# First block of an adaptive-norm layer on one core: conditioning load moved to ScalarE's queue, two engines for the first evacuations, gate product ahead of the low rank product

## Chip, cores, metric

One Trainium2 chip, one core. The metric is the device time of one execution in microseconds (us); lower is better. A time is the median over several executions, and beside it one execution is profiled.

## What is computed

A transformer layer on 2048 tokens of width 256 in float32: a modulation vector from the conditioning vector `c`, gated linear attention, then a mixture of 8 experts with 2 per token and a shared expert. Cut to what bears on the change:

```python
mod = (silu(c) @ wmod).reshape(2, 6, 1, -1)          # c: 2 x 256, wmod: 256 x 1536
sa, ca, ga, sb, cb, gb = mod[:, 0], ..., mod[:, 5]
h = layernorm(x) * (1 + ca) + sa                      # x: 2 x 1024 x 256
q, k, v = h @ Wq, h @ Wk, h @ Wv
gk = log_sigmoid(h @ Wg1 @ Wg2 + bg2) / 16            # low rank: 256 -> 16 -> 256
o = scan over chunks of 64 tokens with decay exp(cumsum(gk))
o = rmsnorm(o) * silu(h @ Wgate)
x = x + ga * (o @ Wo)
h = layernorm(x) * (1 + cb) + sb
x = x + gb * (top-2 experts of h + gated shared expert of h)
```

## The kernel before, in words

It is written by hand, engine by engine: each engine has its own list of instructions in a fixed order, and semaphores tie the lists together. Nothing schedules at run time, and each engine takes its list strictly in order.

The attention half runs over four blocks of 512 tokens (s = 0 to 3; channels lie on the partitions, in two halves of 128, and tokens on the free axis). The change touches only what comes ahead of and in block 0:

- SyncE's queue issues the loads: `x` of block 0 (L439), the conditioning vector into `csb` (L440), the first 512 columns of `wmod` into `hs` (L441), then the small weights `wg` (L444 to L448), `wgate`, `wv`, `wk`, `wq` (L452) and so on.
- TensorE starts with 14 products of a matrix of ones (`idle_products`, L1534), whose results nobody reads. Then `mod_cols` (L1544) makes the modulation columns, `transpose_x` (L1676, XT) turns the normalised rows, three more products of ones follow, and then, in the order of the list: `low_rank` (L1685, LR), the first half of the gate product (L1526, G 0), `gate_logits` (L1693, Z), the second half of the gate product (L1526, G 1), the first half of the values (L1667, V), keys (K), queries (Q), `mod_rows` (L1553), the second half of the values, `key_rows` (L1706), the transposes of block 1.
- ScalarE makes `csil`, the silu of the conditioning vector (L712), the rstd of the layer norm (L726, L728), evacuates both halves of the transposed rows to `hT` with scale and shift (`evac_xT`, L769), evacuates LR to `tT` (L783), takes |z| of Z (L789), softplus (L794, L796), loads the silu table (L718), evacuates G to `sg` (L853), loads another table (L715), evacuates values (L760), makes the gate's exponentials (L802, L806), the normalised rows of block 1 (L775), evacuates `mod_rows` (L734), values (L760), `ktok` (L902), and then `hT` of block 1 (L769).
- VectorE computes statistics (L1065 to L1070), the normalised rows `xn` (L1079), the modulation columns (L1094, L1095), then min(z, 0) (L1207), the log of the gate and its running sum (L1212 to L1219), twice, the statistics of block 1, `kh` (L1326), `nmr` of block 1 (L1333), the queries times the gate (L1340).

Eight PSUM banks are given out by a fixed list, `unit_order`. A unit (XT, LR, G, Z, ...) is one use of a bank; TensorE counts `unit_full` up when it has filled one, in the order of that list, and waits ahead of a unit for what `released` names for the unit that had the bank before. Banks 0 and 1 of the list are `work`, 2 and 3 are `at_ps2` and `at_ps3`, 4 and 5 are `at_ps0` and `at_ps1`.

Of the kernel before, what the change touches and what calls it, by code (L numbers as in the profile page):

```python
# [19 lines left out]
ALU = mybir.AluOpType  # L20
ACT = mybir.ActivationFunctionType
AX_X = mybir.AxisListType.X

P = 128
# [8 lines left out]
KC = HID // P  # L33
# [31 lines left out]
BANKS = {("G", 0): 0, ("G", 1): 1, ("V", 0): 0, ("HT", 0): 0, ("HT", 1): 0, ("K", 0): 1, ("RT", 0): 0, ("RX", 0): 0, ("K", 1): 2,  # L65
         ("Q", 0): 3, ("Q", 1): 1, ("V", 1): 0, ("KT", 0): 2, ("KT", 1): 3, ("XT", 0): 1, ("XT", 1): 0, ("WO", 0): 2,
         ("LR", 0): 3, ("WO", 1): 1, ("Z", 0): 2, ("Z", 1): 3}
# [2 lines left out]
MASK_ORDER = (2, 3, 0, 1)  # L70


FIRST_BANKS = {("V", 0): 4, ("K", 0): 5}


TAIL_BANKS = {1: (3, 2), 2: (4, 5), 3: (0, 1), 4: (3, 2), 5: (4,)}


def unit_order():
    units = [(("MODC", 0, 0), 2), (("XT", 0, 0), BANKS["XT", 0]), (("XT", 0, 1), BANKS["XT", 1])]  # L80
    ring = [2]

    def put(kind, blk, j):
        own = FIRST_BANKS if blk == 0 else {}
        units.append(((kind, blk, j), own.get((kind, j), BANKS[kind, j])))

    def turn(*keys):
        for key in keys:
            units.append((key, (units[-1][1] + 1) % ring[-1]))

    def part(kind, blk, i):
        turn(*([("SD", blk, 0), ("SD", blk, 1)] if kind == "D" else [("SA", blk, i)] + [("SB", blk, i)][:i < FTS - 1]))

    def fill(s, place):
        for kind, blk, i in FILL.get((s, place), ()):
            part(kind, blk, i)

    put("LR", 0, 0)
    put("G", 0, 0)
    put("Z", 0, 0)  # L100
    put("Z", 0, 1)
    put("G", 0, 1)
    for s in range(NBLK):
        b, h = s - 1, s - 2
        if s:
            put("G", s, 0)
            put("G", s, 1)
        put("V", s, 0)
        put("K", s, 0)
        if h >= 0:  # L110
            put("HT", h, 0)
        put("K", s, 1)
        if h >= 0:
            put("HT", h, 1)
            put("RT", h, 0)
        put("Q", s, 0)
        if h >= 0:
            put("RX", h, 0)
        for kind, j in (("Q", 1), ("V", 1), ("KT", 0), ("KT", 1)):
            put(kind, s, j)  # L120
        if s + 1 < NBLK:
            put("XT", s + 1, 0)
            put("XT", s + 1, 1)
        if b >= 0:
            put("WO", b, 0)
        if s + 1 < NBLK:
            put("LR", s + 1, 0)
            put("Z", s + 1, 0)
            put("Z", s + 1, 1)
        if b >= 0:  # L130
            put("WO", b, 1)
    fill(NBLK, "gates")
    fill(NBLK, "half")
    turn(("HT", NBLK - 2, 0), ("HT", NBLK - 2, 1), ("RT", NBLK - 2, 0))
    fill(NBLK, "second")
    turn(("RX", NBLK - 2, 0), ("RK", 0, 0))
    ring.append(4)
    fill(NBLK, "norm")
    turn(("WO", NBLK - 1, 0), ("WO", NBLK - 1, 1))
    fill(NBLK, "stats")  # L140
    fill(NBLK, "ln")
    turn(("HT", NBLK - 1, 0), ("HT", NBLK - 1, 1))
    fill(NBLK, "transposed")
    turn(("RT", NBLK - 1, 0), ("RX", NBLK - 1, 0))
    fill(NBLK, "top2")
    fill(NBLK, "scatter")
    for f in range(EARLY_UP, FTS):
        units += [((kind, NBLK - 1, f), TAIL_BANKS[f][n]) for n, kind in enumerate(("SA", "SB")[:1 + (f < FTS - 1)])]
    units += [(("SD", NBLK - 1, n), n) for n in range(2)]
    return units  # L150
# [25 lines left out]
def adaln_moe(nc, x, cT, wmod, wq, wk, wv, wg1, wg2, bg2, wgate, norm_w, wo,  # L176
              router, e_up, e_down, s_up, s_down, out):
    with ExitStack() as ctx:
# [6 lines left out]
        def sem(name):  # L185
            return ctx.enter_context(nc.semaphore(name))
# [7 lines left out]
        at_ps = [ps(f"at_ps{j}", [P, 512]) for j in range(NPAIR)]  # L194
        o_ps = [ps("o_even", [P, 512]), ps("o_odd", [P, 512])]
# [150 lines left out]
        xs_zero = sem("xs_zero")  # L346
        ones_ready = sem("ones_ready")
        const_pool, ident_ready, zero_ready, kv_full = sem("const_pool"), sem("ident_ready"), sem("zero_ready"), sem("kv_full")
        modf_ready, mod_stored, ld_rows = sem("modf_ready"), sem("mod_stored"), sem("ld_rows")
        unit_full, modr_full, nmr_ready, ld_modr = sem("unit_full"), sem("modr_full"), sem("nmr_ready"), sem("ld_modr")  # L350
        dve_step, act_step, pool_step = sem("dve_step"), sem("act_step"), sem("pool_step")
# [38 lines left out]
        def released(key):  # L390

            kind, blk, j = key
            return {
                "MODC": [(modc_ready, 2)],
                "XT": [(ht_ready, 2 * blk + j + 1)],
                "LR": [(tt_ready, blk + 1)],
                "Z": [(zabs_done, 2 * blk + j + 1), (zmin_done, 2 * blk + j + 1)],
                "G": [(sg_ready, 2 * blk + j + 1)],
                "V": [(v_ready, 2 * blk + j + 1)],
                "K": [(kh_ready, 2 * blk + j + 1)],  # L400
                "WO": [(woev_done, 2 * blk + j + 1)],
                "Q": [(qeo_ready, 4 * blk + 2 * j + 2)],
                "KT": [(ktok_ready, 2 * blk + j + 1)],
                "HT": [(h2T_ready, 2 * blk + j + 1)],
                "RT": [(rt_ready, blk + 1)],
                "RX": [(logit_ready, blk + 1)],
                "RK": [(rank_read, 2)],
                "SA": [(silu_done, FTS * blk + j + 1)] if j < FTS - 1 else [(hs_ready, FTS * blk + j + 1)],
                "SB": [(hs_ready, FTS * blk + j + 1)],
                "SD": [(shev_done, 2 * blk + j + 1)],  # L410
            }[kind]

        def bank(key):
            return (work + at_ps[2:] + at_ps[:2])[BANK_OF[key]]

        def wait_unit(eng, key):

            eng.wait_ge(unit_full, TURN[key] + 1)
# [18 lines left out]
        @block.sync  # L437
        def _(sp):
            sp.dma_start(x_sb[:, 0:TPB, :], x[0:BLK, :].rearrange("(t p) c -> p t c", p=P)).then_inc(ld_x[0], 16)  # L439
            sp.dma_start(csb[:, :, :], cT).then_inc(ld_c, 16)  # L440
            sp.dma_start(wmod_sb[:, :, 0:2 * HID], wmod.rearrange("(k p) n -> p k n", p=P)[:, :, 0:2 * HID]  # L441
                         ).then_inc(ld_mod, 16)
            sp.wait_ge(zero_ready, 4)
# [264 lines left out]
        def _(act):  # L708
            a = nc.scalar
            steps = Steps(act, act_step)  # L710
            act.wait_ge(ld_c, 16)
            a.activation(csil[:, :, :], csb[:, :, :], ACT.Silu).then_inc(csil_ready, 1)  # L712

# [51 lines left out]
            def evac_xT(s):  # L765
                row = s // BPB
                for k in range(KC):
                    wait_unit(act, ("XT", s, k))
                    a.activation(hT[:, k, :], bank(("XT", s, k))[:, :], ACT.Identity,  # L769
                                 bias=cols[:, 0, k, row:row + 1], scale=cols[:, 1, k, row:row + 1]).then_inc(ht_ready, 1)  # L770
# [64 lines left out]
                a.activation(dtop[:, tl, :], dtop[:, tl, :], ACT.Copy).then_inc(pexp_ready, 1)  # L835

            act.wait_ge(modc_ready, 2)
            evac_xT(0)
            evac_low_rank(0)
            z_abs(0)  # L840
            for s in range(NBLK + 1):
# [216 lines left out]
        def _(dve):  # L1058
# [201 lines left out]
            def next_state(s):  # L1260
# [17 lines left out]
                if s >= 1:  # L1278
# [3 lines left out]
                                     kv_in[:, :, :, :].rearrange("p g v c -> p (g v c)"), 0.0,  # L1282
                                     ALU.mult, ALU.add).then_inc(state_ready, 1)

            dve.wait_ge(const_pool, 1)
            z_min(0)
            for s in range(NBLK + 1):
# [225 lines left out]
        def _(pe):  # L1513
            t_ = nc.tensor

            def begin(key):

                if LAST_IN_BANK[key]:
                    for s, val in released(LAST_IN_BANK[key]):
                        pe.wait_ge(s, val)  # L1520
                return bank(key)

            def project(key, w, gr, rhs):
                o = begin(key)
                for k in range(KC):
                    ins = t_.matmul(o[:, :], w[:, k, gr * P:(gr + 1) * P], rhs[:, k, :],  # L1526
                                    start=(k == 0), stop=(k == KC - 1))
                ins.then_inc(unit_full, 1)


            def idle_products(n):

                for _ in range(n):
                    t_.matmul(at_ps[0][:, 0:P], ones[:, :], ones[:, :], start=True, stop=True)  # L1534

            def mod_cols():
                pe.wait_ge(csil_ready, 1)
# [139 lines left out]
                    ins.then_inc(unit_full, 1)  # L1677

            def low_rank(s):
                pe.wait_ge(ht_ready, 2 * s + 2)  # L1680
                o = begin(("LR", s, 0))
                for gr in range(KC):
                    for k in range(KC):
                        r = slice(32 * (2 * gr + k), 32 * (2 * gr + k) + 32)
                        ins = t_.matmul(o[r, :], wg1_sb[:, k, :], hT[:, k, :], start=True, stop=True)  # L1685
                ins.then_inc(unit_full, 1)
# [54 lines left out]
            mod_cols()  # L1741
            transpose_x(0)
            idle_products(3)
            pe.wait_ge(ld_wg, 16 * (NPAIR + 3))
            low_rank(0)
            pe.wait_ge(ld_wgate, 16)
            project(("G", 0, 0), wgate_sb, 0, hT)
            gate_logits(0)
            project(("G", 0, 1), wgate_sb, 1, hT)
            for s in range(NBLK + 1):  # L1750
                b, h = s - 1, s - 2
                if b >= 0:
# [237 lines left out]
```

## Times and profile before

| what | value |
|---|---|
| median of 3 runs | 378.75 us (377.57 to 380.47) |
| profiled execution, its own time | 378.7 us |
| its span, first to last instruction | 376.9 us |
| what lies around the span | 1.8 us |
| TensorE busy | 360.6 us, 96% of the span |
| VectorE busy | 237.4 us, 63% |
| ScalarE busy | 144.6 us, 38% |
| GpSimd busy | 147.7 us, 39% |
| chain that ended last, by engine | TensorE 79%, VectorE 12%, ScalarE 5%, issue 3% |
| granted TensorE clock, mean | 0.999 of 2.4 GHz |

The busy shares are averages over the whole kernel. The change acts in the first 31 us, and what it is worth is read there: what each engine waits for in that stretch, and what hands over to the next block.

### The profile page before, as it was taken

Reading aid. Unit: us, or ns where it says so; the run is one execution under the profiler, and the core shown is the slowest. Engines: PE = TensorE matmul, PEld = TensorE weight load, DVE = VectorE, ACT = ScalarE, POOL = GpSimd, SP = SyncE. Lnnn points to the kernel's source line nnn. Section 1 sums busy time; section 2 is a strip of 40 time slices with the busy share of each in tenths; the row PEclk is TensorE's granted clock in tenths of the full one; section 3 lists DMA queues with packets and bytes.
Section 4 is the critical chain, followed back from the end, with each engine's and each line's share of the span. In section 5 each row is a group of like instructions: output and inputs, shape, how many; then the busy total and the mean of one; then the engine's idle time right before and its main releaser. Section 6 shows DMA issues by size and latency. Waiting matters only on the chain.

```text
span 376.9 us, 10005 instructions
## 1 busy us (share of the span) xinstructions
PE 360.6 (96%) x3871; PEld 226.8 (60%) x3872; DVE 237.4 (63%) x578; ACT 144.6 (38%) x303; POOL 147.7 (39%) x253
## 2 busy tenths in 40 slices
PE   8999989989899989899999999999999999999994
PEld 8445656665665564556744844756666666665463
DVE  4199576996799479664491771165565555555295
ACT  3597556716681613271052411024333333331110
POOL 7705007101510242026270075333667666675100
PEclk9999999999999999999999999999999999999999
DMA  6970200000000000069920082422333333211495
GB/s 204 337 236 27 92 4 3 2 5 3 2 2 5 2 2 4 3 175 333 297 99 14 1 213 80 124 72 87 107 93 111 113 102 92 70 57 44 154 353 172
DMA packets 29902, 36.68 MB, mean 97 GB/s; under 512 B 4567, under 2 KB 26530, under 8 KB 29860
## 3 DMA queue, kind: packets, MB, share of 16 engines
q1 hardware_dynamic: 26452, 27.58, 24.2%
q0 software_dynamic: 3408, 8.51, 6.7%
q8 instruction: 30, 0.49, 0.5%
q14 instruction: 12, 0.10, 0.1%
HBM read 23.31 MB, written 13.68 MB: 98 GB/s over the span
## 4 chain that ended last, share of the span: by engine, by line
PE 79%; DVE 12%; ACT 5%; issue 3%; DVEq 0%; POOL 0%; ACTq 0%; POOLq 0%
PE at_ps L1864 13%; PE work L1477 10%; PE at_ps L1477 8%; PE at_ps L1492 6%; PE work L1887 4%; PE at_ps L1526 4%; PE work L1492 3%; PE work L1889 3%; PE work L1526 2%; PE at_ps L1848 2%; PE at_ps L1699 2%; DVE arena L1227 2%; PE at_ps L1534 2%; PE at_ps L1717 2%; PE work L1667 2%
## 5 line engine op out<-in xcount | busy, mean ns | idle before, releaser
L678 POOL DMA_INDIRECT ys_tokens<-er_pos,goal_u x39 | 42.1, 1080 | 33.8 <-DVE er_pos L1400 27.2
L1864 PE MATMUL at_ps<-arena 128*128 x156 | 54.5, 472 | 0.0
L649 POOL DMA_INDIRECT xs_sorted<-h2tok,pos_u x32 | 31.9, 997 | 37.2 <-DVE pos_u L1024 18.8
L607 POOL TENSOR_TENSOR sq<-sq,sg 128x512 f32<-128x512 f32 x8 | 10.0, 1274 | 88.8 <-issue 88.8
L1864 PEld LDWEIGHTS at_ps<-arena 128*128 128x128 f32 x156 | 26.6, 190 | 14.9 <-issue 6.6
L930 ACT ACTIVATE arena<-at_ps 128x176 f32<-128x176 f32 x39 | 12.4, 318 | 58.8 <-PE at_ps L1864 58.8
L1400 DVE SCALAR_TENSOR_TENSOR er_pos<-work,goal,sq 128x256 f32<-128x256 f32 x39 | 17.2, 480 | 22.0 <-PE work L1894 21.0
L1477 PE MATMUL work<-h2T,sup_sb 128*128 128x512 f32 x56 | 25.7, 598 | 0.2 <-ACT hs L699 0.2
L1380 DVE TENSOR_TENSOR arena<-at_ps,arena 128x176 f32<-128x176 f32 x39 | 13.3, 342 | 18.4 <-ACT arena L930 15.9
L1227 DVE COPY_PREDICATED arena<-causal,at_ps 128x512 f32<-128x512 uint32 x32 | 20.5, 720 | 4.0 <-PE at_ps L1564 4.0
L1492 PE MATMUL at_ps<-sdn_sb,hs 128*128 128x256 f32 x100 | 22.1, 380 | 0.0
L1123 DVE TENSOR_TENSOR hs<-work,hs 128x512 f32<-128x512 f32 x12 | 8.3, 689 | 20.6 <-PE work L1477 20.6
L1492 PEld LDWEIGHTS at_ps<-sdn_sb,hs 128*128 128x128 f32 x100 | 18.9, 190 | 3.4 <-issue 1.0
L699 ACT ACTIVATE hs<-at_ps 128x512 f32<-128x512 f32 x9 | 5.4, 597 | 39.9 <-PE at_ps L1477 39.9
L926 ACT ACTIVATE arena<-at_ps 128x256 f32<-128x256 f32 x39 | 14.9, 384 | 9.7 <-PE at_ps L1848 9.3
L1477 PEld LDWEIGHTS work<-h2T,sup_sb 128*128 128x128 f32 x56 | 10.3, 190 | 12.2 <-issue 11.8
L1393 DVE SCALAR_TENSOR_TENSOR sq<-sq,goal,rows 128x256 f32<-128x256 f32 x40 | 17.4, 478 | 0.0
L1848 PEld LDWEIGHTS at_ps<-ident,h2tok 128*128 128x128 f32 x78 | 10.8, 141 | 10.0 <-issue 6.1
L1526 PE MATMUL work<-hT,wgate_sb 128*128 128x512 f32 x32 | 14.9, 602 | 0.0
L1848 PE MATMUL at_ps<-ident,h2tok 128*128 128x128 f32 x78 | 14.8, 273 | 0.0
L611 POOL TENSOR_TENSOR arena<-arena 128x512 f32<-128x512 f32 x8 | 10.2, 1283 | 11.6 <-DVE arena L1340 11.4
L1667 PE MATMUL work<-wv_sb,hT 128*128 128x256 f32 x56 | 13.6, 386 | 0.5 <-ACT sg L853 0.5
(287 smaller groups left out, 815.0 us busy)
## 6 DMA issues: line engine op xcount, KB each, us to landing
h2tok<-xs_sorted SPq DMA_DIRECT2D x40, 131.5 KB, 2.1
arena<-ys_tokens SPq DMA_DIRECT2D x8, 512.0 KB, 7.4
arena<-in_e_up SPq DMA_DIRECT2D x8, 352.0 KB, 5.4
x_sb<-in_x SPq DMA_DIRECT2D x4, 512.0 KB, 8.5
out_rows<-x_sb SPq DMA_DIRECT2D x16, 128.0 KB, 4.2
sup_sb<-in_s_up SPq DMA_DIRECT2D x2, 640.0 KB, 4.9
xs_sorted<-state SPq DMA_DIRECT2D x2, 526.0 KB, 14.4
xs_sorted<-state SPq DMA_DIRECT2D x8, 131.5 KB, 4.3
```

The lines of the kernel that those rows point to most:

```text
L649: g.indirect_dma_start(out=xs_dram, out_offset=bass.IndirectOffsetOnAxis(ap=pos_u[:, k, t:t + 1], axis=0), in_=h2tok[:, t, :], in_offset=N ...
L678: g.indirect_dma_start(out=ys_dram, out_offset=bass.IndirectOffsetOnAxis(ap=goal_u[:, i:i + 1], axis=0), in_=yout[:, q % 2, u, :], in_offs ...
L1227: v.copy_predicated(atm[:, n % 2, j, :], causal[:, :, :].bitcast(U32).rearrange("p r l -> p (r l)"), at_ps[j][:, :]).then_inc(atm_ready, 1)
L1393: v.scalar_tensor_tensor(out=row_gain[:, t, :], in0=row_step, scalar=goal[:, (u // 2) % XPAIRS, t, 2:3], in1=rows[:, 0, GB, :], op0=ALU.mu ...
L1400: v.scalar_tensor_tensor(out=yout[:, (u // 2) % 2, u % 2, :], in0=work[u % 2][:, 0:HID], scalar=goal[:, (u // 2) % XPAIRS, u % 2, 1:2], in ...
L1477: ins = t_.matmul(o[0:m, :], sup_sb[:, k, w, f0:f0 + m], h2T_of[blk][:, k, :], start=(k == 0), stop=(k == KC - 1))
L1492: t_.matmul(o[jj][:, t * HID:(t + 1) * HID], hs[:, f, tk], sdn_sb[:, f, :], start=(t == 0 and f == 0), stop=False, skip_group_check=True)
L1526: ins = t_.matmul(o[:, :], w[:, k, gr * P:(gr + 1) * P], rhs[:, k, :], start=(k == 0), stop=(k == KC - 1))
L1667: ins = t_.matmul(o[:, t * HID:(t + 1) * HID], hT[:, k, tk], wv_sb[:, k, :], start=(k == 0), stop=(k == KC - 1))
L1848: ins = t_.transpose(at_ps[u % 2][:, k * P:(k + 1) * P], xt[:, u // 2, u % 2, k * P:(k + 1) * P], ident[:, :])
L1864: ins = t_.matmul(at_ps[2 + u % 2][:, 0:2 * FE], xT[:, u % 2, k * P:(k + 1) * P], eup[:, bass.ds(e, 1), k, :].rearrange("p a n -> p (a n)" ...
L1887: t_.matmul(work[t][:, 0:HID], hTe[:, w % 2, t * P:(t + 1) * P], main[:, bass.ds(e[t], 1), :].rearrange("p a n -> p (a n)"), start=True, s ...
```

## The change

Five things are edited. (1) The load of the conditioning vector leaves SyncE's queue and becomes ScalarE's first instruction. (2) The transposes of block 0 go to banks 4 and 5 (`at_ps0`, `at_ps1`), and the products of ones write `o_ps[1]`. (3) Channel half 0 of `hT` is evacuated by ScalarE as before, half 1 by VectorE, each with a semaphore of its own (`ht_first`). (4) TensorE makes G 0 first, each of its two matmuls waiting for its own half of `hT`, then LR. (5) G 1 now stands between LR and Z, where G 0 stood. The counts of `ht_ready` are lowered by two, since block 0 no longer raises it.

```diff
-FIRST_BANKS = {("V", 0): 4, ("K", 0): 5}
+FIRST_BANKS = {("V", 0): 4, ("K", 0): 5, ("XT", 0): 4, ("XT", 1): 5}
...
+    put("G", 0, 0)
     put("LR", 0, 0)
-    put("G", 0, 0)
+    put("G", 0, 1)
     put("Z", 0, 0)
     put("Z", 0, 1)
-    put("G", 0, 1)
...
-                "XT": [(ht_ready, 2 * blk + j + 1)],
+                "XT": [(ht_ready, 2 * blk + j - 1) if blk else (ht_first[j % KC], 1)],
...
-            sp.dma_start(csb[:, :, :], cT).then_inc(ld_c, 16)
...
+            act.dma_start(csb[:, :, :], cT).then_inc(ld_c, 16)
             act.wait_ge(ld_c, 16)
...
             act.wait_ge(modc_ready, 2)
-            evac_xT(0)
+            wait_unit(act, ("XT", 0, 0))
+            a.activation(hT[:, 0, :], bank(("XT", 0, 0))[:, :], ACT.Identity,
+                         bias=cols[:, 0, 0, 0:1], scale=cols[:, 1, 0, 0:1]).then_inc(ht_first[0], 1)
...
+            dve.wait_ge(modc_ready, 2)
+            wait_unit(dve, ("XT", 0, 1))
+            v.tensor_scalar(hT[:, 1, :], bank(("XT", 0, 1))[:, :], cols[:, 1, 1, 0:1], cols[:, 0, 1, 0:1],
+                            ALU.mult, ALU.add).then_inc(ht_first[1], 1)
             dve.wait_ge(const_pool, 1)
...
-                    t_.matmul(at_ps[0][:, 0:P], ones[:, :], ones[:, :], start=True, stop=True)
+                    t_.matmul(o_ps[1][:, 0:P], ones[:, :], ones[:, :], start=True, stop=True)
...
-                pe.wait_ge(ht_ready, 2 * s + 2)
+                if s:
+                    pe.wait_ge(ht_ready, 2 * s)
...
             idle_products(3)
+            pe.wait_ge(ld_wgate, 16)
+            o = begin(("G", 0, 0))
+            for k in range(KC):
+                pe.wait_ge(ht_first[k], 1)
+                ins = t_.matmul(o[:, :], wgate_sb[:, k, 0:P], hT[:, k, :], start=(k == 0), stop=(k == KC - 1))
+            ins.then_inc(unit_full, 1)
             pe.wait_ge(ld_wg, 16 * (NPAIR + 3))
             low_rank(0)
-            pe.wait_ge(ld_wgate, 16)
-            project(("G", 0, 0), wgate_sb, 0, hT)
+            project(("G", 0, 1), wgate_sb, 1, hT)
             gate_logits(0)
-            project(("G", 0, 1), wgate_sb, 1, hT)
```

TensorE's list behind the transposes, before; `wg1_sb` marks LR, `wgate_sb` the gate product, `tT` Z:

```order
L1534 MATMUL at_ps0<-ones 128x128 x3
L1685 MATMUL at_ps3<-hT,wg1_sb 32x512 [waits ht_ready,ld_wg]
L1685 MATMUL at_ps3<-hT,wg1_sb 32x512 x3
L1526 MATMUL work0<-hT,wgate_sb 128x512 [waits ht_ready,ld_wgate]
L1526 MATMUL work0<-hT,wgate_sb 128x512
L1693 MATMUL at_ps2<-tT,wg2_sb 128x512 [waits tt_ready,modc_ready]
L1693 MATMUL at_ps3<-tT,wg2_sb 128x512
L1526 MATMUL work1<-hT,wgate_sb 128x512 [waits ht_ready]
L1526 MATMUL work1<-hT,wgate_sb 128x512
```

The same place in the changed kernel, down to the first product of the values:

```order
L1541 MATMUL o_odd<-ones 128x128 x3
L1756 MATMUL work0<-hT,wgate_sb 128x512 [waits ht_first0,ld_wgate]
L1756 MATMUL work0<-hT,wgate_sb 128x512 [waits ht_first1]
L1693 MATMUL at_ps3<-hT,wg1_sb 32x512 [waits ld_wg]
L1693 MATMUL at_ps3<-hT,wg1_sb 32x512 x3
L1533 MATMUL work1<-hT,wgate_sb 128x512 x2
L1701 MATMUL at_ps2<-tT,wg2_sb 128x512 [waits tt_ready,modc_ready]
L1701 MATMUL at_ps3<-tT,wg2_sb 128x512
L1674 MATMUL at_ps0<-wv_sb,hT 128x256 [waits ht_first0,ld_wv]
```

Between the evacuation of the transposes and Z stood four matmuls of LR and two of the gate product; now four of LR and four of the gate product stand there.

VectorE's list at the same place, before:

```order
L1094 COPY cols<-at_ps2 128x4 [waits unit_full,dve_step]
L1095 TENSOR_SCALAR cols<-at_ps2 128x4
L1207 TENSOR_SCALAR gate_pair<-at_ps2 128x512 [waits zabs_done,unit_full,const_pool]
L1207 TENSOR_SCALAR gate_pair<-at_ps3 128x512 [waits zabs_done,unit_full]
L1212 TENSOR_TENSOR gate_pair<-gate_pair,za 128x512 [waits zmin_done,zln_done]
```

And in the changed kernel:

```order
L1097 COPY cols<-at_ps2 128x4 [waits unit_full,dve_step]
L1098 TENSOR_SCALAR cols<-at_ps2 128x4
L1290 TENSOR_SCALAR hT<-at_ps1,cols 128x512 [waits unit_full,modc_ready]
L1210 TENSOR_SCALAR gate_pair<-at_ps2 128x512 [waits zabs_done,unit_full,const_pool]
L1210 TENSOR_SCALAR gate_pair<-at_ps3 128x512 [waits zabs_done,unit_full]
L1215 TENSOR_TENSOR gate_pair<-gate_pair,za 128x512 [waits zmin_done,zln_done]
```

One instruction is added, between the modulation columns and the first work on Z.

## Rows read from the trace of the kernel before

**Rows 1.** Chain that ended last, first 33 us: start us, us, what
```profile
1.02 6.32 PE at_ps L1534 x28
...
26.76 1.94 PE work L1667 x8
...
28.72 0.66 ACT arena L760 x2
...
30.36 1.34 ACT hT L769 x2
...
31.75 1.11 PE at_ps L1685 x8
```

**Rows 2.** Timeline 6.5 to 17 us: start, us, engine, line, operation, count [idle before]
```profile
6.95 1.99 PEld L1544 LDWEIGHTS at_ps<-csil,hs 128*128 128x128 f32 x16
...
7.06 1.43 DVE L1079 TENSOR_SCALAR xn<-x_sb,rstd,nmr 128x256 f32<-128x256 f32 x4
...
8.89 1.07 PE L1676 MATMUL work<-ident,xn 128*128 128x128 f32 x8
...
9.62 1.45 ACT L769 ACTIVATE hT<-work,cols 128x512 f32<-128x512 f32 x2 [2.79 <-PE work L1676]
...
11.21 1.06 PE L1685 MATMUL at_ps<-hT,wg_sb 128*32 128x512 f32 x8 [0.58 <-ACT hT L769]
...
12.21 1.98 PE L1526 MATMUL work<-hT,wgate_sb 128*128 128x512 f32 x4
...
14.12 1.13 PE L1693 MATMUL at_ps<-tT,wg_sb 64*128 64x512 f32 x4
...
15.18 1.98 PE L1526 MATMUL work<-hT,wgate_sb 128*128 128x512 f32 x4
15.28 1.09 ACT L789 ACTIVATE za<-at_ps 128x512 f32<-128x512 f32 x2 [2.26 <-PE at_ps L1693]
...
17.00 1.89 PE L1667 MATMUL at_ps<-wv_sb,hT 128*128 128x256 f32 x8
```

**Rows 3.** Waits of ScalarE, all there are from 16.2 to 32 us: in total, times, longest
```profile
ACT xn L775 <- DVE nmr L1333: 0.6, 1, 0.6
ACT arena L760 <- PE work L1667: 0.2, 1, 0.2
```

**Rows 4.** Timeline of VectorE (first row) and ScalarE, 15 to 32 us
```profile
18.58 0.69 DVE L1212 TENSOR_TENSOR gate_pair<-gate_pair,za 128x512 f32<-128x512 f32 x1 [1.28 <-ACT za L796]
...
26.22 2.08 ACT L775 ACTIVATE xn<-x_sb,nmr,rstd 128x256 f32<-128x256 f32 x4 [0.59 <-DVE nmr L1333]
...
28.20 0.36 ACT L734 ACTIVATE yT<-o_even 128x256 f32<-128x256 f32 x1
...
28.72 0.66 ACT L760 ACTIVATE arena<-work 128x256 f32<-128x256 f32 x2 [0.16 <-PE work L1667]
```

**Rows 5.** Line L1207 alone, 15 to 18 us: duration ns min/median/max
```profile
L1207 DVE TENSOR_SCALAR gate_pair<-at_ps x2: 679/685/691, 16.0 to 16.6; 128x512 f32<-128x512 f32 x2
```

**Rows 6.** Timeline 0 to 7 us: what waits for the first loads
```profile
4.22 1.40 DVE L1065 BATCH_NORM_STATS2 stats<-x_sb 128x6 f32<-128x256 f32 x4 [4.22 <-DMA x_sb<-in_x]
...
4.43 0.20 ACT L712 ACTIVATE csil<-csb 128x4 f32<-128x4 f32 x1 [2.38 <-DMA csb<-in_cT]
...
6.29 0.30 ACT L726 ACTIVATE lnv<-mv,eps_c 128x4 f32<-128x4 f32 x1 [0.35 <-DVE mv L1070]
```

**Rows 7.** DMA issues of the first 8 us: engine, count, KB, us to landing
```profile
hs<-in_wmod SPq DMA_DIRECT2D x1, 512.0 KB, 5.0
```

**Rows 8.** Timeline: SyncE's queue at its second and third issue
```profile
1.27 0.49 SPq L440 DMA_DIRECT2D csb<-in_cT  x1
...
1.82 0.43 SPq L441 DMA_DIRECT2D hs<-in_wmod  x1
```

**Rows 9.** Stretches: length; busy us (instructions) by engine; clock; DMA share; GB/s
```profile
3.00:4.00 1.00, 1.00 (x7) 1.00 (x7) 0.00 (x0) 0.00 (x0) 0.93 (x4) 1.00 1.04 293
...
17.00:30.00 13.00, 13.00 (x63) 7.84 (x62) 11.37 (x26) 12.13 (x25) 2.35 (x2) 1.00 0.69 201
```

More of the change, by code:

```diff
@@ L70 @@
 MASK_ORDER = (2, 3, 0, 1)
-FIRST_BANKS = {("V", 0): 4, ("K", 0): 5}
+FIRST_BANKS = {("V", 0): 4, ("K", 0): 5, ("XT", 0): 4, ("XT", 1): 5}
 TAIL_BANKS = {1: (3, 2), 2: (4, 5), 3: (0, 1), 4: (3, 2), 5: (4,)}
 def unit_order():
-    units = [(("MODC", 0, 0), 2), (("XT", 0, 0), BANKS["XT", 0]), (("XT", 0, 1), BANKS["XT", 1])]
+    units = [(("MODC", 0, 0), 2), (("XT", 0, 0), 4), (("XT", 0, 1), 5)]
     ring = [2]
@@ L348, in adaln_moe @@
         const_pool, ident_ready, zero_ready, kv_full = sem("const_pool"), sem("ident_ready"), sem("zero_ready"), sem("kv_full")
+        ht_first = [sem("ht_first0"), sem("ht_first1")]
         modf_ready, mod_stored, ld_rows = sem("modf_ready"), sem("mod_stored"), sem("ld_rows")
```

## Prediction

> **What bounds the kernel now.** I read the chain that ended last first, and only its first 32 us, since nothing behind block 0 is edited. It begins on TensorE with the products of ones, is TensorE at the end of the second half of the values (26.76 + 1.94 = 28.70 us), and there it passes to ScalarE: values, `ktok`, `hT` of block 1, done at 31.70 us, and LR of block 1 starts at 31.75 [rows 1]. A reader of the chain alone would say: TensorE bounds block 0, so whatever starts TensorE sooner is gained.
>
> The second view is the list of waits from 16.2 to 32 us, and it says how thin that reading is. ScalarE's wait for TensorE at the handover is 0.16 us; its only other one is for VectorE's `nmr`, 0.59 us, and VectorE's last one is for ScalarE's softplus (1.28 us, over at 18.58) [rows 3, 4]. In the stretch 17 to 30 us TensorE is busy for 13.00 of 13.00 us, ScalarE for 12.13 and VectorE for 11.37 [rows 9]. So there are two strings of nearly equal length through block 0. One is TensorE's own queue. The other starts at Z: |z| on ScalarE at 15.28, right behind Z's end at 15.25, two softplus steps, VectorE at 18.58, straight on to `nmr`, then ScalarE's rows of block 1 (26.22 to 28.30), `mod_rows` (to 28.56), and then the handover at 28.72 [rows 2, 4]. The second string is only 0.16 us shorter than the first. It hangs on when Z is done, not on when TensorE is done.
>
> **The change part by part.**
>
> *Conditioning load on ScalarE's queue.* SyncE issues `wmod` at about 1.27 instead of 1.82 us [rows 8]: 0.55 us sooner. Before, it lands at 1.82 + 5.0 = 6.8 us [rows 7, 8], while the weight loads of the 14 products of ones (28 instructions) hold TensorE's queue from 1.02 to 6.95 us, 5.93 / 28 = 0.212 us each with no gap, and the modulation product's first weight load follows at 6.95 [rows 1, 2]. The queue hides the landing, and it is unchanged in length: 0 us gained (an earlier landing would count only with fewer products of ones ahead of it). The issue on ScalarE (0.49 us on SyncE [rows 8]) stands ahead of its table load; `csil` was made at 4.43, and ScalarE then had 0.35 us to spare ahead of `lnv` [rows 6]. The vector would have to land 0.35 us later than now to cost anything, and it is issued about 0.5 us sooner. 0 us.
>
> *Evacuation by two engines.* ScalarE took 9.62 to 11.07 for both halves, and LR started at 11.21, 0.14 us behind [rows 1, 2]. One half alone is (1.45 us for two that overlap a little) about 0.77 us, done at 10.39 to 10.41. VectorE's half has no row; the nearest is its 128x512 read of PSUM in L1207, 0.685 us [rows 5]. The second transpose ends at 9.96 [rows 2], VectorE has been idle since the modulation columns, so half 1 is done at about 10.7. Bounds of this operation: 0.68 us if the two scalars per partition cost nothing, 0.77 us as on ScalarE; in both cases it is done ahead of 11.3 us, when TensorE wants it (below). So the first product can start at 10.40 + 0.14 = 10.55 us, 0.66 us sooner than LR did.
>
> *G 0 ahead of LR, G 1 ahead of Z.* TensorE's starts are the prices: LR 11.21 to 12.21 = 1.00 us, G 0 12.21 to 14.12 = 1.91, Z 14.12 to 15.18 = 1.06, G 1 15.18 to 17.00 = 1.82 [rows 2]. From the first product to Z's start it was 1.00 + 1.91 = 2.91 us. Now it is 1.91 + 1.00 + 1.91 = 4.82. A full-width product followed by LR (four strips of 32 columns) has no row here; bounds are 1.82 (full width followed by full width) and 1.91 (full width followed by Z), and I take 1.91. So:
>
> - Z starts at 10.55 + 4.82 = 15.37 instead of 14.12: **1.25 us later**. `tT` is no bound: LR ends at 12.46 + 1.06 = 13.5, and an evacuation of the size of ScalarE's 0.77 us makes 14.3.
> - V starts at 15.37 + 1.06 = 16.43 instead of 17.00: **0.57 us sooner**. All four units are still ahead of it, so this is the 0.66 us less 0.09 for one more change of shape.
>
> *Where both arrive.* TensorE's string is at the handover 0.57 us sooner, at 28.13. The other string is 1.25 us later all along: |z| at 16.53, VectorE at 19.83, the rows of block 1 27.47 to 29.55, `mod_rows` to 29.81, and so values at about 29.83 instead of 28.72. The 0.16 us wait for TensorE is gone and is all the slack there was: 1.25 - 0.16 + 0.02 = **1.1 us later**. Everything behind it, `ktok`, `hT`, LR of block 1, is ScalarE at work without a pause, and TensorE waits there for it already [rows 1]. What else is late next: TensorE's transposes of block 1 need the rows of block 1, which are done at 29.55, and take 1.07 us as in block 0 [rows 2], so they end at 30.7, while ScalarE wants the first of them at 30.36 + 1.1 = 31.5. Hidden by 0.8 us.
>
> *Behind block 0.* The order there is the same, each block starts from the last one's `hT`, and the loads it needs were early. I take the 1.1 us to pass to the end. Sum against the profiled execution: 376.9 + 1.1 = 378.0 us of span, 379.8 of time; that execution (378.7) lies at the median (378.75), so **379.85 us**.
>
> *New banks, one semaphore for each half.* V's first half now waits for the bank of the transposes, free since 10.4, at 16.4: 0 us. G 0 no longer has a unit ahead of it in its bank. 0 us.
>
> **The rivals.**
>
> 1. *TensorE's string sets the end (faster).* If the string behind Z had as much slack as it loses, 1.25 us, block 0 would end with TensorE, 0.57 us sooner: 378.2 us. For it: the chain names TensorE up to 28.70, and TensorE is the engine that is never idle. Against it: waits of 0.16 and 0.59 us are all that the trace shows, and the 0.59 us is ScalarE waiting for VectorE, on the same string. It decides from a slack of about 1.1 us on.
> 2. *The delay is absorbed further on (no change).* Blocks 2 and 3 and the expert half have stretches in which TensorE's queue is full; a later handover in block 1 may meet one that is bound by TensorE work which is not late. For it: 96% busy. Against: the chain passes through ScalarE from 28.72 to 31.70 [rows 1], so TensorE's own queue is pushed back by the 1.1 us at that point. 378.8 us.
> 3. *The first rows land later (slower still).* From 3 to 4 us the DMA engines are busy all the time (share 1.04), and VectorE's first work waits for `x` at 4.22 [rows 6, 9]. From `x` the way goes to `xn`, done at 7.06 + 1.43 = 8.49, and the transposes start at 8.89 [rows 2], right behind the modulation products, so 0.40 us are to spare. With `wmod` 0.55 us sooner beside it, `x` can be late by up to 0.55 us, and 0.15 us would be left; if the transposes' weight loads are what the rows must meet, 0.1 us more: 380.1 us.
>
> The Trainium skill, page "DMA: Bandwidth & Descriptors", section "Issuing engines are not separate DMA queues", says that transfers issued by different engines run on the same 16 DMA engines and interleave, and that a second issuing engine only saves the time of the issue. By that rule the move takes nothing off the transfers and can hold up `x`, as the third rival has it; by the rows alone the move is worth 0.
>
> **How the numbers follow.** Forecast (0.7 to 1.6 us slower, 379.45 to 380.35): 0.60. Rival 1: 0.12. Rival 2: 0.15. Rival 3: 0.13. The three runs before span 377.57 to 380.47, so a median moves by some 0.8 us by itself. The range goes from 378.0 (takes in most of rivals 1 and 2) to 381.2 (rival 3 and 1 us of spread). All cases lie within 1% (3.8 us), which is about what a measurement of this kernel can tell from no change; only a mechanism that I don't see would leave it: faster 0.02, within 1% 0.94, slower 0.04.
>
> **What would show it.** In the profile after: G 0 starts at about 10.55 us and runs into its second matmul without a pause; Z starts at about 15.4; |z| at about 16.5; V at about 16.4; ScalarE's second evacuation of values (L760's) at about 29.8, with no wait for TensorE ahead of it, and the chain going from there back through `mod_rows`, the rows of block 1, VectorE and softplus to Z instead of through TensorE; LR of block 1 at about 32.85 instead of 31.75. The prediction is wrong if ScalarE still waits for TensorE at that handover, if Z starts before 15 us, or if LR of block 1 is late by 1.1 us and the span isn't.

## The result, and the profile after

The changed kernel takes 379.9 us (median of 19 runs, 378.46 to 381.77), the kernel before 378.57 us in 19 runs beside it: ratio 1.0034, 95% interval 1.0019 to 1.0049. A second set gave 379.87 against 378.57 us, ratio 1.0030 (1.0011 to 1.0050). The change makes the kernel 1.3 us slower, 0.34%; 379.85 was forecast.

| profiled execution | before | after |
|---|---|---|
| span | 376.9 us | 380.0 us |
| TensorE busy | 360.6 us | 362.6 us |
| VectorE busy | 237.4 us | 237.8 us |
| ScalarE busy | 144.6 us | 143.8 us |
| mean granted TensorE clock, of 2.4 GHz | 0.999 | 0.993 |
| chain by engine | PE 79%, DVE 12%, ACT 5% | PE 74%, DVE 14%, ACT 6% |

This one execution is longer by 3.1 us, more than the medians, and its clock column says why to look twice. The timeline of the changed kernel, as in [rows 2, 6] (start us, length us, engine, line, operation, [idle before, releaser]):

```profile
0.78 0.44 ACTq L711 DMA_DIRECT2D csb<-in_cT  x1
...
4.75 1.41 DVE L1068 BATCH_NORM_STATS2 stats<-x_sb 128x6 f32<-128x256 f32 x4 [4.75 <-DMA x_sb<-in_x]
...
6.48 1.85 PE L1551 MATMUL at_ps<-csil,hs 128*128 128x2 f32 x16
...
9.03 1.92 PE L1683 MATMUL at_ps<-ident,xn 128*128 128x128 f32 x8 [0.71 <-DVE xn L1082]
...
12.02 2.14 PE L1756 MATMUL work<-hT,wgate_sb 128*128 128x512 f32 x4
...
17.00 1.13 PE L1701 MATMUL at_ps<-tT,wg_sb 64*128 64x512 f32 x4
...
18.06 1.99 PE L1674 MATMUL at_ps<-wv_sb,hT 128*128 128x256 f32 x8
```

`x` lands at 4.75 instead of 4.22 us; TensorE is through with its modulation products at 8.33 and has nothing to do until 9.03, when `xn` is there; and the transposes take 1.92 us, where they took 1.07. The stretches around it (length, busy time and count of each engine, granted clock, DMA share, GB/s):

```profile
8.00:9.00 1.00, 0.32 (x3) 0.23 (x3) 1.00 (x6) 0.00 (x0) 0.83 (x3) 1.00 0.69 176
9.00:10.00 1.00, 0.97 (x5) 0.97 (x6) 0.11 (x2) 0.00 (x0) 0.84 (x4) 0.56 1.09 372
```

From 9.1 us on the clock is granted at 1.2 GHz (0.50 in the half microseconds from 9.5 to 12), behind TensorE's pause. This comes ahead of the first product whose place was changed, so the new order didn't cause it, and it isn't in every execution: of the changed kernel's 19 runs 14 have a mean clock of 0.993 to 0.997 (median span 378.3 us), five have 0.998 or more (376.9 us).

The other half is as forecast. The waits from 16 to 33 us, to be held against [rows 3]:

```profile
PE work L1683 <- DVE arena L1347: 0.8, 1, 0.8
ACT xn L776 <- DVE nmr L1340: 0.6, 1, 0.6
```

ScalarE no longer waits for TensorE at the handover. TensorE waits there, for VectorE, and the chain that ended last goes through ScalarE and VectorE where it went through TensorE [rows 1]:

```profile
17.07 1.11 PE at_ps L1701 x4
18.18 1.07 ACT za L790 x2
...
28.91 0.16 DVE nmr L1340
29.10 2.08 ACT xn L776 x4
31.17 0.27 ACT yT L735
31.44 0.54 ACT arena L761 x2
31.98 0.97 ACT xn L905 x2
32.95 1.35 ACT hT L770 x2
34.34 1.11 PE at_ps L1693 x8
```

LR of block 1 starts at 34.34 instead of 31.75 us, 2.59 us later.

### The profile page after: what moved, and what is told of

Same layout as the page of the kernel before. It is cut to its first block, busy times and chain, and to the rows that moved or that the text cites. A ratio compares the mean times of both kernels' runs of the same rounds, so it can differ in the third digit from the quotient of the medians.

```text
span 380.0 us, 10007 instructions
## 1 busy us (share of the span) xinstructions
PE 362.6 (95%) x3871; PEld 227.7 (60%) x3872; DVE 237.8 (63%) x579; ACT 143.8 (38%) x302; POOL 147.7 (39%) x253
## 4 chain that ended last, share of the span: by engine, by line
PE 74%; DVE 14%; ACT 6%; issue 4%; DMA 1%; DVEq 0%; ACTq 0%
PE at_ps L1876 13%; PE work L1484 10%; PE at_ps L1484 8%; PE at_ps L1499 6%; PE work L1899 4%; PE work L1499 3%; PE work L1901 3%; PE at_ps L1533 2%; PE at_ps L1860 2%; PE at_ps L1707 2%; DVE arena L1230 2%; DVE stats L1068 2%; PE at_ps L1725 2%; PE work L1533 1%; PE o_even L1627 1%
## 5 line engine op out<-in xcount | busy, mean ns | idle before, releaser
L1068 DVE BATCH_NORM_STATS2 stats<-x_sb 128x6 f32<-128x256 f32 x32 | 11.2, 411 | 4.9 <-DMA x_sb<-in_x 4.7
```

The lines of the kernel that those rows point to most:

```text
L1068: steps.did(v.bn_stats(stats[:, which, t, :], x_sb[:, tile0 + t, :]))
```

## The experiments

There were twelve experiments, in three sets (e1 to e4, e5 to e8, e9 to e12); some are the same kernel a second time. Those of one set share a chip and the runs of the kernel before beside them (medians 378.25, 378.57 and 378.13 us), and each ratio is to these. "17" means 17 instead of 14 products of ones ahead of the modulation products. The last two columns sort the executions by their mean granted clock, as printed to three places; they carry much of what follows. The mean doesn't say where the clock fell; only the profiles do. In some profiles it is also at half in the last one or two microseconds of the span, behind the last product, where it costs nothing.

| kernel | load on | evacuation | order | ones | median us | spans with clock 0.998+ | with less |
|---|---|---|---|---|---|---|---|
| before, three sets | SyncE | ScalarE | old | 14 | 378.1 to 378.6 | 376.0 to 376.1 (54 of 96) | 377.0 to 377.5 (42 of 96) |
| changed, first runs | ScalarE | two | new | 14 | 379.90 | 376.9 (5 of 19) | 378.3 (14 of 19) |
| e5_changed_again | ScalarE | two | new | 14 | 379.87 | 376.6 (4 of 9) | 378.3 (5 of 9) |
| e1_load_only | ScalarE | ScalarE | old | 14 | 378.21 | 376.2 (7 of 12) | 377.2 (5 of 12) |
| e2_no_load | SyncE | two | new | 14 | 378.78 | 376.7 (8 of 12) | 378.35 (4 of 12) |
| e3_split_only | SyncE | two | old | 14 | 377.88 | 375.7 (8 of 12) | 377.3 (4 of 12) |
| e4_more_ones | ScalarE | two | new | 17 | 378.28 | 376.4 (12 of 12) | none |
| e9_changed_17 | ScalarE | two | new | 17 | 378.54 | 376.7 (12 of 12) | none |
| e10_split_load_17 | ScalarE | two | old | 17 | 377.06 | 375.3 (12 of 12) | none |
| e7_split_17 | SyncE | two | old | 17 | 377.04 | 375.25 (6 of 6) | none |
| e11_split_17_again | SyncE | two | old | 17 | 376.70 | 374.9 (12 of 12) | none |
| e6_before_17 | SyncE | ScalarE | old | 17 | 377.30 | 375.5 (12 of 12) | none |
| e12_before_17_again | SyncE | ScalarE | old | 17 | 377.24 | 375.4 (12 of 12) | none |
| e8_z_last | SyncE | ScalarE | LR, G 0, G 1, Z | 17 | 378.79 | 377.0 (11 of 12) | 378.0 (1 of 12) |

**e1_load_only.** The kernel before with one edit:

```diff
-            sp.dma_start(csb[:, :, :], cT).then_inc(ld_c, 16)
...
+            act.dma_start(csb[:, :, :], cT).then_inc(ld_c, 16)
             act.wait_ge(ld_c, 16)
```

> The kernel before, with only the load of the conditioning vector moved to ScalarE's queue. Theory A (a late x and a slow clock): x of block 0 lands at about 4.7 us instead of 4.2, TensorE stands idle ahead of the transposes for about 0.5 to 0.7 us, in most executions its clock then falls to 1.2 GHz for a while, the first LR starts later than 11.21 us by 0.2 (clock kept) to 1.4 us (clock lost), and the time is 0.2 to 1.3 us above that of the kernel before. Theory B (only the order of the products costs anything, as the prediction had it): LR starts at 11.2 us and the time is that of the kernel before within 0.2 us.

Measured: 378.21 us, ratio 0.9997 (0.9979 to 1.0015). Its profile has `x` at 4.29 us, no pause of TensorE, and LR at 11.16. By itself the move costs nothing that these runs can tell, as the prediction had it; the products of ones ran until 7.3 us in this execution, so the landing of `wmod` stayed hidden behind them.

**e2_no_load.** The changed kernel with the load back on SyncE's queue.

> The changed kernel, with the conditioning vector's load back on SyncE's queue. Theory B, the prediction's own sum: first gate product at 10.55 us, Z at 15.37 us, LR of block 1 at 32.85 us (before: 31.75), time 1.1 us above that of the kernel before. Theory A: the whole loss of the changed kernel comes from the late x and the clock, so LR of block 1 starts at 31.75 us or sooner and the time is at most that of the kernel before.

Measured: 378.78 us, ratio 1.0014 (0.9993 to 1.0036): half of the loss, with an interval that reaches both theories. Where the clock holds its span is 376.7 against 376.1 us, and that speaks against theory A: something is lost with the clock held, too. Its profile shows a second way into the same trouble (timeline of TensorE, then a stretch):

```profile
7.07 1.92 PE L1551 MATMUL at_ps<-csil,hs 128*128 128x2 f32 x16 [0.46 <-DMA hs<-in_wmod]
8.84 1.77 PE L1683 MATMUL at_ps<-ident,xn 128*128 128x128 f32 x8
```

```profile
9.00:10.00 1.00, 1.00 (x7) 1.00 (x7) 0.23 (x2) 0.14 (x1) 0.92 (x3) 0.53 0.82 192
```

Here the products of ones end at 6.6 us, TensorE waits 0.46 us for `wmod`, and the clock falls at 9 us. So the loss of clock doesn't need the moved load. LR of block 1 started at 34.12 in this profile, 2.37 us later than in the kernel before; held against 32.57 in e5 below, where the clock held, about 1.55 us of that are the slow stretch.

**e3_split_only.** The changed kernel with the load on SyncE's queue and the old order of products, LR waiting for both halves. TensorE's list, `+` marking what the kernel before hasn't got:

```diff
+            for k in range(KC):
+                pe.wait_ge(ht_first[k], 1)
             low_rank(0)
             pe.wait_ge(ld_wgate, 16)
             project(("G", 0, 0), wgate_sb, 0, hT)
             gate_logits(0)
             project(("G", 0, 1), wgate_sb, 1, hT)
```

> Only the two-engine evacuation and its banks: the vector's load on SyncE's queue and the products in the order of the kernel before (LR, G 0, Z, G 1). Theory B: LR of block 0 waits for VectorE's half, starts at about 10.85 us instead of 11.21, everything behind it shifts by the same 0.36 us (Z at 13.76, LR of block 1 at 31.4), time 0.36 us below that of the kernel before. Rival: TensorE's three products of ones behind the transposes, or the second evacuation, keep LR at 11.1 us or later, and nothing is gained.

Measured: 377.88 us, ratio 0.9982 (0.9957 to 1.0007). Where the clock holds its span is 375.7 against 376.1 us. The sign is as expected, but the interval of the ratio includes no change at all; e11's profile tells more. The profile of e3 is one of those with a fall of the clock.

**e4_more_ones.** The changed kernel, `idle_products(14)` made `idle_products(17)`.

> The changed kernel, with 17 instead of 14 products of ones ahead of the modulation products, about 0.64 us more of work at 2.4 GHz, to fill the pause in which TensorE waited for xn in the changed kernel's profile (8.3 to 9.03 us). Theory A (the pause costs the clock): the granted clock stays at 1.00 behind 9 us, the first gate product starts at 10.7 us or so instead of 12.02, and the time falls by about 1 us against the changed kernel's 1.3 us above before. Rival (the fall of the clock has nothing to do with this pause): the clock falls as often, and three more products change nothing or add up to 0.3 us.

Measured: 378.28 us, ratio 0.9990 (0.9972 to 1.0008). None of its 12 executions has a clock under 0.998, where 19 of 28 of the changed kernel have. Its first gate product starts at 10.96 us instead of 12.02, and its transposes start right behind the modulation products. With three more products, and no pause ahead of the transposes, the clock holds; whether it is the missing pause or the added work that holds it, no run tells apart.

**e5_changed_again.**

> The changed kernel once more, on the chip of the runs beside it, since its single profile had a fall of TensorE's clock at 9 us. If the fall is a matter of chance that the change makes likelier, most executions have a mean granted clock of 0.993 to 0.996 and a span of about 378.3 us, the others 0.998 to 1.000 and about 376.9. Time 1.0 to 1.5 us above before.

Measured: 379.87 us, ratio 1.0030 (1.0011 to 1.0050): five executions of nine with the lower clock, four without. Its profile fell among those where the clock held, and so is the one to check the prediction's times by. Timeline:

```profile
4.50 1.41 DVE L1068 BATCH_NORM_STATS2 stats<-x_sb 128x6 f32<-128x256 f32 x4 [4.50 <-DMA x_sb<-in_x]
...
6.08 1.92 PE L1551 MATMUL at_ps<-csil,hs 128*128 128x2 f32 x16 [0.21 <-DMA hs<-in_wmod]
...
8.77 1.09 PE L1683 MATMUL at_ps<-ident,xn 128*128 128x128 f32 x8 [0.77 <-DVE xn L1082]
...
10.45 1.95 PE L1756 MATMUL work<-hT,wgate_sb 128*128 128x512 f32 x4
...
15.24 1.13 PE L1701 MATMUL at_ps<-tT,wg_sb 64*128 64x512 f32 x4
16.30 1.99 PE L1674 MATMUL at_ps<-wv_sb,hT 128*128 128x256 f32 x8
16.40 1.09 ACT L790 ACTIVATE za<-at_ps 128x512 f32<-128x512 f32 x2 [2.25 <-PE at_ps L1701]
...
27.33 2.07 ACT L776 ACTIVATE xn<-x_sb,nmr,rstd 128x256 f32<-128x256 f32 x4 [0.59 <-DVE nmr L1340]
29.31 0.36 ACT L735 ACTIVATE yT<-o_even 128x256 f32<-128x256 f32 x1
29.58 0.63 ACT L761 ACTIVATE arena<-work 128x256 f32<-128x256 f32 x2
...
32.57 1.07 PE L1693 MATMUL at_ps<-hT,wg_sb 128*32 128x512 f32 x8 [0.58 <-ACT hT L770]
```

TensorE paused here for 0.77 us too, and kept its clock. So a pause alone doesn't settle it.

**e6_before_17.** The kernel before with 17 products of ones.

> The kernel before with 17 instead of 14 products of ones ahead of the modulation products. If a pause of TensorE ahead of the modulation products or the transposes is what costs the clock, all executions have a mean clock of 0.998 or more, none has 0.995; three more products delay the transposes by 0.3 to 0.5 us, so the span is about 376.5 us in all of them (before: 376.1 where the clock holds, 377.5 where it falls), and the median equals that of before within 0.3 us. Rival (the clock falls for another reason): one in three executions still has 0.995.

Measured: 377.30 us, ratio 0.9971 (0.9957 to 0.9986), 12 of 12 with the clock held. It is faster than expected by about 1 us. In this execution all 34 instructions took 5.86 us, less than the 28 of [rows 1], but that is chance: in e12, the same kernel, they took 6.89 us, and LR of block 1 started at 32.32 us, later than in the kernel before. The median falls by 1.3 us here and by 0.9 us in e12. Not all of it is the clock: among executions that keep the clock the span is 375.4 to 375.5 us with 17 products and 376.0 to 376.1 with 14, and no run says where these 0.6 us come from.

**e7_split_17.** e3 with 17 products.

> The two-engine evacuation in the old order (LR first), load on SyncE's queue, with 17 products of ones. If the two effects add: clock held in all executions, LR of block 1 at about 31.8 us, span about 376.1 us, median 0.4 us below that of before_17 and about 0.2 to 0.4 below before. Rival: with the transposes later, the split saves nothing, and it equals before_17.

Measured: 377.04 us (only 6 runs), ratio 0.9961 (0.9948 to 0.9975), the clock held in all 6; 0.3 us below e6, which lies within what the runs scatter by. LR waits 0.40 us for VectorE's half in it, as in e11 below.

**e8_z_last.** The prediction's ledger by itself: e6 with one pair of lines exchanged (and their bank units).

```diff
-            gate_logits(0)
             project(("G", 0, 1), wgate_sb, 1, hT)
+            gate_logits(0)
```

> The kernel before with 17 products of ones and one more edit: G 1 ahead of Z (LR, G 0, G 1, Z). Against before_17 only Z moves, later by the 1.82 us that G 1 takes; everything TensorE does behind both stands where it stood. The prediction's ledger: 1.82 - 0.16 = 1.66 us later at LR of block 1, all of it passed to the end: span 1.7 us above before_17. Rival (part is absorbed behind block 0): LR of block 1 is late by 1.66 us, and the span by 1.1 us or less.

Measured: 378.79 us, 1.5 us above e6 (mean difference 1.6, interval 1.1 to 2.0). Timeline of e8:

```profile
8.86 1.07 PE L1676 MATMUL work<-ident,xn 128*128 128x128 f32 x8
...
15.81 1.13 PE L1693 MATMUL at_ps<-tT,wg_sb 64*128 64x512 f32 x4
16.87 1.99 PE L1667 MATMUL at_ps<-wv_sb,hT 128*128 128x256 f32 x8
...
29.88 0.36 ACT L734 ACTIVATE yT<-o_even 128x256 f32<-128x256 f32 x1
30.15 0.63 ACT L760 ACTIVATE arena<-work 128x256 f32<-128x256 f32 x2
...
33.14 1.07 PE L1685 MATMUL at_ps<-hT,wg_sb 128*32 128x512 f32 x8 [0.58 <-ACT hT L769]
```

and of e6:

```profile
8.71 1.09 PE L1676 MATMUL work<-ident,xn 128*128 128x128 f32 x8
...
13.96 1.13 PE L1693 MATMUL at_ps<-tT,wg_sb 64*128 64x512 f32 x4
...
16.84 1.89 PE L1667 MATMUL at_ps<-wv_sb,hT 128*128 128x256 f32 x8
...
28.56 0.66 ACT L760 ACTIVATE arena<-work 128x256 f32<-128x256 f32 x2 [0.16 <-PE work L1667]
...
31.59 1.06 PE L1685 MATMUL at_ps<-hT,wg_sb 128*32 128x512 f32 x8 [0.58 <-ACT hT L769]
```

Read from the transposes: Z starts 6.95 us behind them instead of 5.25, 1.70 later. V starts 8.01 behind them instead of 8.13: TensorE's own string isn't late at all, and ScalarE's wait for TensorE ahead of the values is gone. LR of block 1 starts 24.28 us behind them instead of 22.88, 1.40 later. So a delay of Z alone, with TensorE on time, arrives less 0.3 us of slack, and the kernel's time shows no further loss of it: 1.6 us, interval 1.1 to 2.0. The rival (1.1 us or less) lies at the very edge of that interval.

**e9 to e12.** Four kernels on one chip, all with 17 products, each one edit from the next.

> The changed kernel with 17 products of ones, beside the three kernels below, each one edit away from the next and all with 17. Against the next kernel only the order of the products differs (G 0, LR, G 1, Z instead of LR, G 0, Z, G 1). The ledger: Z later by 1.91 us less what LR waits more for the second half (0.2 to 0.3), less the slack of 0.16 to 0.25: 1.3 to 1.5 us above split_load_17. Rival (half of it is absorbed further on, as one earlier comparison across kernels suggested): 0.4 to 0.8 us.

> LR first, two-engine evacuation, load on ScalarE's queue, 17 products of ones. Against split_17 only the load's queue differs. If the move is worth nothing once TensorE's queue hides wmod: the same within 0.2 us. Rival (x lands later through it): up to 0.5 us slower.

> The two-engine evacuation in the old order, load on SyncE's queue, 17 products of ones, once more. 0.3 us below before_17 (0.45 us less for evacuation, less 0.1 to 0.15 for the three products of ones that TensorE must end first), about 1.5 us below the kernel before with 14.

> The kernel before with 17 products of ones, once more: 1.0 to 1.3 us below the kernel before with 14, clock of 0.998 or more in all executions.

Measured, with intervals for the difference of the means of 12 runs each, resampled from the listed times:

| step | difference of medians | of means (95%) |
|---|---|---|
| new order (e9 less e10) | +1.5 us | +1.3 (0.8 to 1.8) |
| load on ScalarE's queue (e10 less e11) | +0.4 | +0.2 (-0.4 to 0.7) |
| two-engine evacuation (e11 less e12) | -0.5 | -0.4 (-0.8 to 0.1) |
| all three (e9 less e12) | +1.3 | +1.1 (0.7 to 1.5) |
| three more products (e12 less before) | -0.9 | -1.1 (-1.5 to -0.8) |

The order is shown; the load's 0.4 and the evacuation's gain are within what the runs scatter by. What the evacuation gains is better read in the profile of e11 (the two evacuations, then LR of block 0 and of block 1):

```profile
8.69 1.07 PE L1683 MATMUL at_ps<-ident,xn 128*128 128x128 f32 x8
...
9.87 0.81 DVE L1290 TENSOR_SCALAR hT<-at_ps,cols 128x512 f32<-128x512 f32 x1 [0.70 <-PE at_ps L1683]
...
10.83 1.06 PE L1693 MATMUL at_ps<-hT,wg_sb 128*32 128x512 f32 x8 [0.40 <-DVE hT L1290]
...
31.36 1.06 PE L1693 MATMUL at_ps<-hT,wg_sb 128*32 128x512 f32 x8 [0.57 <-ACT hT L770]
```

LR starts 2.14 us behind the start of the transposes; in e6 it was 11.05 - 8.71 = 2.34. The gain is 0.20 us, not the 0.36 that e3's expectation worked out; 0.13 us of the difference is that VectorE's half takes 0.81 us and not 0.68.

**e11 has the lowest median:** 376.70 us, ratio 0.9959 (0.9936 to 0.9982) to the kernel before; the changed kernel has 1.0034, so it is about 0.0075 x 378.5 = 2.8 us below that. It keeps the two-engine evacuation with its banks, undoes the order and the move of the load, and holds the clock. From e10 (ratio 0.9959 too) and e7 (0.9961) it can't be told apart.

## Why the prediction was right, and where it was so by luck

- *Two strings of nearly equal length, and the second hangs on Z.* Right, and shown by e8, where only Z moves and the kernel is 1.5 us slower with TensorE's queue on time.
- *First gate product at 10.55 us, Z at 15.37, V at 16.43, |z| at 16.53.* In the execution where the clock held (e5): 10.45, 15.24, 16.30, 16.40. The sum of the starts, 4.82 us from the first product to Z, measured 4.79. The 1.91 us taken for a full-width product ahead of LR was measured as 12.33 - 10.45 = 1.88.
- *0.16 us of slack at the handover.* Mis-sized. ScalarE's instructions overlap: in e5 the values' evacuation starts at 29.58, while `mod_rows` ends at 29.67. The 0.16 us of waiting and 0.08 of overlap were both to be had. Values came 0.86 us later than at 28.72, not 1.1, and LR of block 1 at 32.57, not 32.85: 0.82 us later, where 1.1 was forecast. Of these 0.28 us, 0.12 are no error of the sum: in e5 the transposes start at 8.77 us, before at 8.89. Counted from the transposes Z is 1.24 us later (1.25 forecast) and LR of block 1 **0.94 us later** (1.1 forecast), so the slack was 0.30 us, where the sum has 0.14. It is 0.30 in e8 against e6 and 0.29 in e9 against e12, too.
- *All of it passes to the end.* Right in size (e8, e9 against e10). One block further it can be read in every profile: from LR of block 1 to LR of block 2 it took 32.30 to 32.37 us in all fourteen, early or late. Further on, single executions hide it: from LR of block 2 to LR of block 3 the same code took 37.0 to 37.8 us.
- *The sum starts from a span of 376.9 us.* Luck. That execution kept its clock, yet lies 0.8 us above the 376.0 to 376.1 of those that do, because its last store was late. SyncE waits for it at the end, in the profile before and in e5's:

```profile
SPq L530 <- DMA out_rows<-x_sb: 2.9, 2, 2.7
...
SPq L530 <- DMA out_rows<-x_sb: 1.4, 2, 0.9
```

  The profile of the changed kernel has the long wait (2.9) as well, the other twelve the short one (1.3 to 1.4). Without these 1.5 us the sum would have started from 375.4; the time beside it, 378.7, happened to lie at a median that is pulled up by executions which lose the clock.
- *Two engines evacuate within 0.68 to 0.77 us each.* VectorE took 0.81 us, outside these bounds. It cost nothing in the changed kernel, whose second matmul wants this half later, and a part of the gain where LR comes first (e11).
- *The load's move is worth 0, with a late `x` as a rival of 0.13.* Right for the kernel before (e1). In the changed kernel `x` was late: waited for until 4.48, 4.50, 4.75 and 4.78 us in its four profiles (e4, e5, the first and e9). But in e1 and e10, with the same load on ScalarE's queue and the old order, it was 4.29 and 4.21, and with the load on SyncE's queue 4.16 to 4.37 in eight profiles. So the runs don't show that the move is what makes `x` late. Where it was late by 0.53 us, the transposes started 0.14 us later (9.03 against 8.89), as the rival priced it; what the rival had no price for was the pause of TensorE ahead of them.
- *What no step named: the clock.* The prediction took the products of ones to hold TensorE's queue to 6.95 us, with `wmod` hidden behind them, as in its one profile. They end anywhere from 5.9 us (e5) to 7.3 us (before): the weight loads of the ones take 333 ns each at first and 192 ns later, and the step between the two came at 4.0 us in e5 and at 7.2 us in the kernel before. What comes after products that end early must wait for `wmod` or `xn`. In three of the four profiles with such a pause (the changed kernel's, e2 and e3, not e5) the clock fell to 1.2 GHz at about 9 us, for about 3 us; the first gate product then starts at 12.02 instead of 10.45. In the ten profiles without a pause ahead of the transposes it didn't fall there. The changed kernel lost it in 19 of 28 executions, the kernel before in 42 of 96, the eight experiments with 17 products in 1 of 90.

So the 1.3 us are, for executions that keep the clock, 0.5 to 0.9 us (spans 376.6 and 376.9 against 376.0 to 376.1), near the 0.82 of LR of block 1; the rest is the clock lost more often and at a higher price, 1.4 to 1.7 us against 0.9 to 1.4. As an estimate from the counts: 19 of 28 times about 1.5 us, less 42 of 96 times about 1.1, is 0.5 us; with the 0.5 to 0.9 us that makes 1.0 to 1.4. Forecast and measurement agree to 0.05 us because a delay that was 0.16 us too large, and a start that fitted by chance, stood in for a loss of clock that was missing. With 17 products, where the clock holds, all three steps come to 1.1 us (0.7 to 1.5), and the profiles of e9 and e12 show 0.92 at LR of block 1, counted from the transposes.

## What to carry to other kernels

When the chain names one engine without a gap, look at the small waits of the others at the next handover: an order that starts the busy engine sooner can still be slower, if it puts the product that the other engines wait for behind more work. Price a reordering by when each result is ready for its reader, not by when the producing engine gets through. And read the granted clock of many executions before believing one profile: filler work that ends early by chance can cost about as much as the edit under test (0.9 to 1.3 us against 1.3 here).

## What the runs showed of the hardware

- The granted-clock column stands at 1.00 from the first instruction, yet the beginning runs at the lower level. These are weight loads of the same ones (ns min/median/max, then when): in the kernel before at 6 us, with 1.00 in the column; in the changed kernel at 11 us, with 0.50; in the kernel before at 10 us, with 1.00:

```profile
L1534 PEld LDWEIGHTS at_ps<-ones x5: 333/333/333, 5.9 to 6.7; 128*128 128x128 f32 x5
...
L1541 PEld LDWEIGHTS o_odd<-ones x6: 333/333/337, 10.5 to 11.6; 128*128 128x128 f32 x6
...
L1534 PEld LDWEIGHTS at_ps<-ones x6: 190/192/192, 9.7 to 10.2; 128*128 128x128 f32 x6
```

- The step from 333 to 192 ns came at 4.0 to 7.2 us in the fourteen profiles, though the first product starts at 1.02 us in all. With 14 products and a step at 5.5 to 5.7 us TensorE then paused and the clock fell (the changed kernel, e2, e3); with 17 and a step at 5.2 to 5.9 us (e7, e8, e10, e11) it had no pause ahead of the transposes, and the clock held.
- The fall came at 9.0 to 9.1 us in all three profiles that have it, with pauses of 0.70 us (ahead of it), 0.46 and 0.26 us (two microseconds ahead of it, in e2 and e3); pauses of 0.21 and 0.77 us in e5 had no fall. For e3:

```profile
8.00:9.00 1.00, 1.00 (x10) 0.95 (x10) 0.80 (x5) 0.00 (x0) 0.75 (x4) 0.99 0.93 217
9.00:10.00 1.00, 1.00 (x7) 1.00 (x6) 0.08 (x2) 0.29 (x1) 0.92 (x3) 0.50 0.89 241
```

- VectorE's evacuation with two scalars per partition took 0.81 us for 128x512 out of PSUM, in all nine profiles that have it; more than the 0.685 of [rows 5], which is one operation with a constant, and more than ScalarE's 0.78 for the other half of the same tile.
- The vector's 2 KB on ScalarE's queue, and `wmod` 0.55 us sooner, came with `x` up to 0.5 us late in the changed kernel, and with `x` on time in e1 and e10. A late `x` is what the Trainium skill, page "DMA: Bandwidth & Descriptors", section "Issuing engines are not separate DMA queues", leads one to expect, since it says that transfers run on the same 16 DMA engines and interleave, whichever engine issued them. Four profiles agree with it and two don't, and they don't tell whether the vector's transfer or the earlier `wmod` was in the way.
